# Turning the second gate's ranks with vector transposes instead of matmul transposes, in fifteen of sixteen tiles

## The reference

```python
# layer 0: cond = x @ w_eff.T (quantised weight plus a low-rank part); ffn = base + top-2-of-8 gated low rank
# layer 1: cond = x @ weight.T + bias + scale * (x @ a_sel.T) @ b_sel.T   (one adapter per sequence)
def _L1_ffn_ref(x, base_W, router_W, lora_A, lora_B):
    base = jnp.einsum('bsd,od->bso', x, base_W)
    logits = jnp.einsum('bsd,ed->bse', x, router_W)
    probs = softmax(logits)
    top_vals, top_idx = jax.lax.top_k(probs, 2)
    w_dense = one_hot(top_idx) weighted by top_vals / sum(top_vals)
    mid = jnp.einsum('bsd,edr->bser', x, lora_A)      # 8 experts x 16 ranks = 128 values a token
    mid = mid * w_dense[..., None]                    # the second gate
    inc = jnp.einsum('bser,erd->bsd', mid, lora_B)
    return base + inc * SCALING
```

## Time and profile before

| what | value |
|---|---|
| median of three runs | 889.35 us |
| the profiled execution | 889.4 us, its span 887.2 us |
| PE busy | 882.7 us, 99% of the span |
| DVE busy | 714.5 us, 81% |
| ACT busy | 324.3 us, 37% |
| POOL busy | 156.5 us, 18% |
| granted TensorE clock | 1.0 throughout |

### The profile page before, as it was taken

The page is one execution under the profiler, slowest core; times in us unless marked ns, Lnnn a source line. Parts: engine busy times, 40 slices in busy tenths (PEclk is TensorE's granted clock), DMA queues, the critical chain, the costliest instruction groups (busy, mean ns, idle before and its releaser), DMA issues.

```text
span 887.2 us, 13623 instructions
## 1 busy us (share of the span) xinstructions
PE 882.7 (99%) x4566; PEld 773.3 (87%) x4566; DVE 714.5 (81%) x1587; ACT 324.3 (37%) x525; POOL 156.5 (18%) x310
## 2 busy tenths in 40 slices
PE   9999999999999999999999999999999999999998
PEld 8999998888998888888888888888888888888787
DVE  6999999786787968989787877877877877877875
ACT  6688878421424434232322222222222222222221
POOL 0210120111011002313202302302302312312300
PEclk9999999999999999999999999999999999999999
DMA  9533340785312042575786887887887987987976
GB/s 349 213 98 114 125 137 25 245 258 174 120 49 95 3 141 76 173 285 209 237 295 252 297 287 259 298 299 245 302 294 248 304 278 261 305 287 252 304 230 233
DMA packets 62609, 191.93 MB, mean 216 GB/s; under 512 B 8256, under 2 KB 12742, under 8 KB 60620
## 3 DMA queue, kind: packets, MB, share of 16 engines
q1 hardware_dynamic: 50282, 158.92, 50.6%
q0 software_dynamic: 11968, 31.88, 12.9%
q10 hardware_dynamic: 290, 0.26, 0.1%
HBM read 158.80 MB, written 32.76 MB: 216 GB/s over the span
## 4 chain that ended last, share of the span: by engine, by line
PE 97%; DMA 2%; SPq 0%; DVE 0%; ACT 0%; issue 0%; DVEq 0%
PE bank L941 16%; PE bank L593 15%; PE bank L594 15%; PE bank L595 15%; PE bank L965 8%; PE bank L923 7%; PE bank L909 5%; PE bank L969 4%; PE bank L1064 2%; PE bank L749 2%; PE bank L918 2%; DMA t_lo<-t_scratch 1%; PE bank L637 1%; PE bank L858 1%; PE bank L644 1%; DMA m_raw<-m1t 1%
## 5 line engine op out<-in xcount | busy, mean ns | idle before, releaser
L941 PE MATMUL bank<-g_hi,xs 128*128 128x512 f32 x440 | 146.9, 395 | 0.0
L556 POOL DMA_DIRECT2D p1sel<-p_scratch x128 | 65.6, 512 | 289.6 <-issue 289.6
L941 PEld LDWEIGHTS bank<-g_hi,xs 128*128 128x128 f32 x440 | 81.7, 188 | 15.7
L965 PE MATMUL bank<-t_hi,xs 128*128 128x512 f32 x336 | 90.9, 392 | 0.0
L941 PE MATMUL bank<-g_lo,xs 128*128 128x512 f32 x220 | 86.7, 394 | 0.0
L1141 ACT ACTIVATE xs<-x_raw 128x1024 fp32r<-128x1024 f32 x60 | 61.8, 1054 | 51.8 <-PE bank L969 50.2
L1514 DVE TENSOR_TENSOR xs<-x_raw,xs 128x1024 fp32r<-128x1024 f32 x60 | 73.2, 1242 | 7.4 <-ACT xs L1141 7.0
L593 PE MATMUL bank<-gx,xs 128*128 128x304 f32 x256 | 78.5, 307 | 0.0
L595 PE MATMUL bank<-gx,xs 128*128 128x304 f32 x256 | 77.4, 302 | 0.0
L594 PE MATMUL bank<-gx,xs 128*128 128x304 f32 x256 | 77.2, 301 | 0.0
L965 PEld LDWEIGHTS bank<-t_hi,xs 128*128 128x128 f32 x336 | 63.0, 188 | 14.3 <-DMA t_hi<-t_scratch 0.3
(11 more groups left out here) (395 smaller groups left out, 2124.3 us busy)
## 6 DMA issues: line engine op xcount, KB each, us to landing
t_hi<-t_scratch SPq DMA_DIRECT2D x82, 512.0 KB, 5.6
t_lo<-t_scratch SPq DMA_DIRECT2D x82, 512.0 KB, 6.5
x_raw<-xq SPq DMA_DIRECT2D x16, 1024.0 KB, 8.6
out<-ost SPq DMA_DIRECT2D x63, 256.0 KB, 8.3
p1sel<-p_scratch POOLq DMA_DIRECT2D x64, 192.0 KB, 6.0
w_raw<-wall SPq DMA_DIRECT2D x15, 512.0 KB, 4.6
w<-e_scratch SPq DMA_DIRECT2D x6, 1024.0 KB, 5.1
ea<-e_scratch POOLq DMA_DIRECT2D x8, 644.0 KB, 5.3
```

Of the source, the lines that this page charges most:

```text
L556: pool.dma_start(f(p1sel[b][64 * s:64 * s + STK, cs]), p1_dram[bass.ds(i * STK, STK), cs]).then_inc(sems[b], 16)
L941: mm = nc.tensor.matmul(bk[j][:], l[:, c, :], m[:, c, :], start=first and c + k == 0, stop=c + k == KH + 1, skip_group_check=True)
L965: nc.tensor.matmul(bk[j][:], x[u][:, c, :], t_hi[:, c, :], start=first and c + u == 0, stop=False, skip_group_check=True)
```

## The change

In tiles 0 to 14 PE no longer turns `midv`. It only waits for `back` (the wait on `mid_s` stays), and goes on to `x_product`. DVE turns `midv` itself, directly after `back`, by a new function `mid_turn`. A vector transpose swaps rows and columns within 32x32 blocks, so a 128x128 block takes 16 of them, block by block; each instruction does both halves of the tile at once (32 partitions, 2 x 32 elements). The result goes to the same PSUM bank `TR`, and the same semaphore `t2_mm` tells ACT. The new function waits for `mid_s`, and in the seven-product tiles for `m0r_s` (ACT's copy of what stood in `TR`). Tile 15 keeps the matmul transposes. In tile 0, `mid_low(0)` now stands between the two halves of `t4_raw`, not behind both. No DMA is issued in another place, and nothing on POOL, SP or ACT is moved.

```diff
-                mid_turn(tau)
+                pe.wait_ge(mid_s, tau + 1)
                 x_product(tau + 1, (0,))
...
+            def mid_turn(tau):
+                v.wait_ge(mid_s, tau + 1)
+                if tau >= REG:
+                    v.wait_ge(m0r_s, tau - REG + 1)
+                turned = TR[:, 0:T2].rearrange("p (b t) -> p b t", b=2)
+                for g in range(P // SX):
+                    ts = slice(SX * g, SX * g + SX)
+                    for k in range(P // SX):
+                        ks = slice(SX * k, SX * k + SX)
+                        ins = nc.vector.transpose(turned[ks, :, ts], midv[ts, :, ks])
+                ins.then_inc(t2_mm, 1)
...
             back(0)
+            mid_turn(0)
             t4_raw(0)
+            mid_low(0)
             t4_raw(1)
-            mid_low(0)
...
             back(1)
+            mid_turn(1)
             s_sums(2)
...
                 back(tau)
+                if tau + 1 < NT2:
+                    mid_turn(tau)
```

More of the change, by code:

```diff
@@ L1118, in _ @@
             low_terms(0, (0, 2, 1, 3))
-            mid_turn(0)
+            pe.wait_ge(mid_s, 1)
             x_product(1)
@@ L1124, in _ @@
             low_terms(1, (0, 2, 1, 3))
-            mid_turn(1)
+            pe.wait_ge(mid_s, 2)
             x_product(2)
```

## The result

| | before | after |
|---|---|---|
| median of the runs, us | 889.17 (888.65 to 889.44, 5 runs) | 900.1 (898.36 to 901.43, 5 runs) |
| profiled execution, span, us | 887.2 | 899.2 |
| its own time, us | 889.4 | 901.43 |

The ratio is 1.012, 95% interval 1.0109 to 1.0131: slower by 10.9 us, where +7.4 was forecast. Three executions in what follows took far longer than all others of the same kernel (3113 us of the SBUF version, 3040 us of the SBUF version for tiles 3 to 14, 1466 us of the kernel before); no median or interval here contains them. The page of the changed kernel: busy time by engine and the chain that ended last, against the earlier trace rows.

A forecast was written before the change was run, and what follows sets the result against it. PE was taken to bound the kernel, busy 99% of the span. -3.15 + 3.5 + 3.5 + 2.4 + 1.2 = +7.4 us gave 896.7 us, slower; own range 893 to 900, wider range 891.5 to 903.5.

The forecast's parts named there:

- PE gains 0.21 us per tile: On PE, dropping the pair of transposes frees 0.21 us in each of fifteen tiles, 3.15 us in all.
- A transpose costs 234 ns; writing to PSUM has no price: On DVE, each new transpose costs 234 ns, PSUM write unpriced; sixteen take 3.98 us, the turn 4.1 us per tile.
- All sixteen are held: In DVE's turn, each transpose changes output partition group and waits for earlier ones to finish; 0.25 us start to start.
- Tile 0 to 1, 3.5 us: DVE has no idle time before `front(1)`, so `m0` is 3.56 us late and PE stalls 3.5 us.
- Tile 1 to 2, 3.5 us: DVE is 4.1 us late at `k_sum`-stage work, ACT's bank 3 copy follows, and PE stalls 3.5 us at tile 2's start.
- the clock rival: TensorE's clock falls to 1.2 GHz after two 3.5 us stalls, for as long as each: +7, 903.7 us; chance 0.07.
- Tile 2 to 3, 2.4 us: DVE's idle 1.32 and 0.39 us leave it 2.4 us late; PE stalls 2.4 us, spread over three places.
- Tiles 3 to 14, 0.1 us each: DVE's 3.87 us idle nearly hides a 4.0 us turn; PE stalls 0.1 us in each of twelve tiles, 1.2 in all.
- that cover: In tiles 3 to 14, DVE's wait for PE's rank product, 2.94 us, which hides the turn.
- unheld transposes: Rival: transposes are not held and follow at 0.14 us, turn 2.3 us; +1.3, 890.7 us; chance 0.09.
- the faster case: Rival: DVE's idle time takes in the whole turn, 1.2 us if transposes cost only columns; -2.0, 887.4 us; chance 0.05.
- dear PSUM writes: Rival: a transpose into PSUM takes 0.29 us, turn 0.67 longer in all fifteen tiles; +10 on top, 906.8 us; chance 0.10.

The follow-up runs named there:

- SBUF version: Changed kernel with the vector transposes writing to an SBUF buffer, `mt`, instead of PSUM bank 5, readers taking it there; 895.94, 896.78 and 897.9 us, ratio 1.0091.
- SBUF version for tiles 3 to 14: Kernel before with the vector turn in tiles 3 to 14 only, written to SBUF buffer `mt`; median 887.24 us, ratio 0.9981.
- one block of sixteen: Changed kernel with only one of the sixteen block transposes per tile, the other fifteen left out; 886.25 us, ratio 0.996.
- split kernel: Changed kernel with each block transpose of 32 x 64 elements split in two of 32 x 32, 32 instructions a tile; one run, 915.8 us.
- the filler: Changed kernel with fourteen extra matmuls, result unread, ahead of PE's wait at tile 2's start; 899.55 us, ratio 1.0112.

## Why the prediction came out as it did

- **PE gains 0.21 us per tile.** Right (one block of sixteen).
- **A transpose costs 234 ns; writing to PSUM has no price.** Wrong, and the step that failed: it rested on an addition into PSUM, 290 ns against 292, and that addition also read PSUM. A transpose pays 21 ns. The rival that named it had 290 ns for one, 56 more than 234, and 10 us for the whole; true were 21 ns, and the SBUF version is faster by 3.3 us in the medians and 5.0 in the profiled executions.
- **All sixteen are held.** Right: 0.27 us from start to start, just the instruction's length and 0.01. By the rule of the Trainium skill that the prediction named ("VectorE: DVE Perf Modes", section "Two Vector instructions with no wait between them") it is the change of group that holds them; the split kernel agrees, 0.10 us within a pair.
- **Tile 0 to 1, 3.5 us.** Measured 3.32 + 0.21 = 3.53. The idle was split as said, ACT's copies first and line 1983 behind it, and the exponential's wait fell from 0.81 to 0.27. That it comes out so near is partly luck: two errors of opposite sign, which these rows show, the kernel before first and then the changed one.

```profile
392.55 0.38 PE L858 MATMUL bank<-pk,ranks_raw 128*128 128x128 f32 x2
```

```profile
379.40 0.42 DVE L2020 TENSOR_TENSOR ranks_raw<-bank,rt 128x256 f32<-128x256 f32 x1
...
391.67 0.17 DVE L1953 COPY rt<-bank 128x16 f32<-128x16 f32 x1
...
396.16 0.20 PEld L858 LDWEIGHTS bank<-pk,ranks_raw 128*128 128x128 f32 x2 [1.82 <-DVE ranks_raw L1983]
```

`front(1)` now starts 391.67 - 379.40 = 12.27 us behind `back(0)` and was 7.90 behind it, so a turn costs DVE 4.37 us here and not 4.1. The slack was read at the weight load (392.32), which ran 0.23 us ahead of its matmul (392.55); once PE waits for `m0`, load and matmul start together (396.16, 396.17). So the slack was 0.23 us larger than the prediction had it, and 3.5 + 0.27 - 0.23 = 3.54. The SBUF version bears this out: its `front(1)` is 11.95 us behind `back(0)`, a turn of 4.05, 3.5 - 0.05 - 0.23 = 3.22, and 3.01 + 0.21 = 3.22 was measured.

- **Tile 1 to 2, 3.5 us.** Measured 5.31. PE starts tile 2 (line 965) at 433.08 and not at 426.10, 6.98 us late where it had been 3.62 late at tile 1's turn: a stall of 3.36 + 0.21 = 3.57, as forecast, and 1.74 more behind that start. The mechanism of the stall was right: ACT's wait for line 2112's `k_raw`, 3.74 us before, is now 4.75 (rows below), and `ost` ends at 433.03. The term lacked the clock, 1.6 of those 1.74 us. That was the clock rival's mechanism, at less than a quarter of its price: the rival had the work of two stalls' length at half speed (+7), while only one stall brought the clock down, and for 3.4 us. The warning that the Trainium skill gives ("TensorE: Matmul & The Clock Gate", section "Why this matters for your kernels") holds here, by the 0.50 in the windows, for this gap of 3.4 us and not for the two of 1.4.

ACT in the changed kernel, at the end of tile 1:

```profile
431.39 0.63 ACT L1141 ACTIVATE k_hi<-k_raw 128x512 fp32r<-128x512 f32 x1 [4.75 <-DVE k_raw L2112]
...
432.45 0.58 ACT L1421 ACTIVATE ost<-bank 128x512 f32<-128x512 f32 x1
```

- **Tile 2 to 3, 2.4 us.** Measured 2.13 + 0.21 = 2.34, in the three places named.
- **Tiles 3 to 14, 0.1 us each.** Measured 0.33 each. The prediction's condition ("where that cover is used up each further 0.1 us of DVE work per tile costs 1.2 us") was right, and the 21 ns used it up: 0.03 us of stall with SBUF and 16 x 0.021 = 0.34 for PSUM make 0.37, near the 0.33 measured. Against the forecast that is 11 x 0.23 = 2.5 us. DVE's wait of 2.94 us before the late `p_sum` sum is gone, as the tile 8 rows of the changed kernel show; for a longer turn that cover is used up:

```profile
663.22 0.70 DVE L1514 TENSOR_TENSOR srk_lo<-ranks_raw,srk_hi 128x128 fp32r<-128x128 f32 x3 [0.33 <-ACT srk_hi L1141]
663.84 0.68 DVE L2245 TENSOR_TENSOR p_sum<-bank,p_sum 128x512 f32<-128x512 f32 x1
```

- **The sum.** +7.4 forecast, +12.0 in the profiled executions: 1.8 of the difference in tile 2 (clock), 2.4 in the steady tiles (PSUM; +1.1 to tile 15 where 12 x -0.11 = -1.3 was forecast), 0.3 already there at tile 0, before any turn of the second gate, which is scatter. The medians differ by 10.9, since the profiled execution was the slowest of the five. The time, 900.1, lies just above the forecast's own range (893 to 900) and inside the wider one, and the loss is where it was put.
- **The range.** 891.5 to 903.5 was said to leave out no more than 2 in 10. By its own chances it leaves out more: unheld transposes (890.7, 0.09), the faster case (0.05) and dear PSUM writes (906.8, 0.10) lie outside, 0.24 together, and the clock's 903.7 (0.07) just outside as well.

One thing stays open: tiles 3 to 14 lose 0.33 us each when the kernel reaches them on time or 10.9 us late (the changed kernel), and 0.21 when tile 2's turn alone has made it 2.5 us late. The forecast's term, with the turn at 4.33 us and the slack larger by 0.23, would be 0.1 + 0.33 - 0.23 = 0.2: that fits the 0.21 and not the 0.33.

## What to carry to other kernels

Before work goes from the bounding engine to another, ask in each stage separately how much idle time the other has there: the same 4.3 us cost 3.5 in a stage where DVE was full and a few tenths where it had 3.9 idle. Where an estimate ends a tenth of a microsecond from the edge and is multiplied by twelve, the price of the destination decides, and an operation of another kind is no measure for it. Read the slack of a wait at the matmul and not at its weight load, which may have run ahead. A stall of the matrix engine can cost more than its length, so read the granted clock behind every idle of some microseconds.

## What the runs showed of the hardware

- A vector transpose of 32 x 64 fp32 elements takes 236 ns into SBUF and 257 into PSUM (240 of each); one of 32 x 32 into PSUM 171 to 233, median 202.
- Transposes one behind the other: 0.27 us apart when the groups of partitions change, 0.10 when they don't (0.31 for a pair less 0.21 for one, if both halves take the same).
- 3.4 us without work brought TensorE's granted clock to its lower level for 3.4 us of the work behind, at a cost of 1.6 us; 1.41 and 1.40 us with 3 us of work between left it at 1.00, and so did 0.24 us behind the filler.
- A weight load can start 0.23 us ahead of its matmul (392.32 and 392.55 in tile 1 of the kernel before). Where PE had waited for the operand, load and matmul started together (396.16 and 396.17).
